# Attention blocks of a two-layer graph kernel on one core: 64-row transposes, another order of scores, context and projections, and three smaller edits

## What is computed

```python
# first layer: attention, then one of eight experts for each node
scores = einsum('bqhd,bkhd->bhqk', q, k) / sqrt(64)
attn = softmax(scores, axis=-1)
o = einsum('bqhk,bkhd->bqhd', attn, v).reshape(b, s, d) @ Wo + bo
h = layernorm(x + o, ln1_g, ln1_b)
probs = softmax(t @ gate_W + gate_b);  idx = argmax(probs);  gw = max(probs)
hid = gelu(einsum('nd,edf->enf', t, W1) + b1)        # 8 experts, 512 -> 2048
out = (einsum('enf,efd->end', hid, W2) + b2)[idx] * gw

# second layer, twice: attention along the edges (a segment softmax per target)
q = ((x @ Wq.T + bq) * 64 ** -0.5);  k = x @ Wk.T;  v = x @ Wv.T
w = segment_softmax(einsum('ehd,ehd->eh', q[tgt], k[src]), tgt)
agg = segment_sum(w * v[src], tgt)
```

## Time and profile before

| | us |
|---|---|
| median of 3 runs | 1137.88 (1135.78 to 1138.45) |
| the profiled execution: device time | 1139.18 |
| the profiled execution: span from first to last instruction | 1137.6 |
| PE busy in the span | 1087.7 |
| first attention, from its first projection | 234.5 to 377.5 |
| experts' loop | 407 to 640 |
| second and third attention | 650.5 to 787.7 and 853.5 to 989 |

### The profile page before, as it was taken

One profiled execution on the slowest core, in us unless ns is written; L12 is line 12 of the kernel. 1 busy time (PEld: TensorE's weight loads), 2 busy tenths in 40 slices (PEclk: granted clock), 3 DMA queues, 4 the chain that ended last, 5 costly groups with the idle time before them and its releaser, 6 DMA issues.

```text
span 1137.6 us, 20475 instructions
## 1 busy us (share of the span) xinstructions
PE 1087.7 (96%) x7489; PEld 733.2 (64%) x7490; DVE 561.7 (49%) x1409; ACT 373.8 (33%) x971; POOL 108.0 (9%) x145
## 2 busy tenths in 40 slices
PE   3899999999999989999999899999999999999999
PEld 2588746468777654455555577887577778755764
DVE  7898867745445422112211445453334555587641
ACT  1112222035455411122212345554124555412630
POOL 1000670020000021001101430000000000001000
PEclk9999999999999989999999999999999999999999
DMA  4100485000000369800799841000210000010001
GB/s 133 38 1 2 117 216 213 1 28 29 20 10 1 149 234 407 346 18 18 310 403 408 292 179 29 29 29 1 74 56 29 29 29 1 1 37 0 1 2 44
DMA packets 21405, 112.73 MB, mean 99 GB/s; under 512 B 5127, under 2 KB 6904, under 8 KB 15198
## 3 DMA queue, kind: packets, MB, share of 16 engines
q1 hardware_dynamic: 15864, 100.95, 23.6%
q0 software_dynamic: 5472, 10.83, 3.8%
HBM read 102.78 MB, written 8.98 MB: 98 GB/s over the span
## 4 chain that ended last, share of the span: by engine, by line
PE 85%; DMA 5%; DVE 4%; issue 3%; ACT 2%; POOL 1%; DVEq 0%; SPq 0%; POOLq 0%
PE psum L623 12%; PE psum L804 10%; PE psum L1003 7%; PE psum L971 6%; PE psum L827 6%; PE psum L858 6%; PE psum L809 5%; PE psum L840 5%; PE psum L691 4%; PE psum L1130 3%; PE psum L1034 3%; PE psum L641 3%; PE psum L1108 3%; DMA arena<-in_moeW 3%; PE psum L761 2%
## 5 line engine op out<-in xcount | busy, mean ns | idle before, releaser
L623 PE MATMUL psum<-arena 128*125 128x512 f32 x320 | 141.6, 599 | 0.8 <-ACT arena L1204 0.7
L1234 ACT ACTIVATE arena<-arena,small 125x625 f32<-125x625 f32 x120 | 97.0, 809 | 90.5 <-DVE small L1625 90.5
L804 PE MATMUL psum<-arena 128*128 128x313 f32 (+1 forms) x384 | 110.0, 435 | 2.3 <-ACT arena L1172 1.4
L1003 PE MATMUL psum<-arena 128*64 128x256 f32 x896 | 103.6, 390 | 5.1 <-DMA arena<-in_moeW 4.6
L623 PEld LDWEIGHTS psum<-arena 128*125 128x125 f32 x320 | 59.8, 190 | 74.7 <-issue 72.0
L1309 ACT ACTIVATE arena<-psum,cols 128x64 f32<-128x64 f32 x224 | 47.5, 363 | 183.8 <-PE psum L985 183.8
L971 PE MATMUL psum<-arena 128*64 128x512 f32 x448 | 99.2, 594 | 3.2 <-DMA arena<-in_moeW 2.2
L804 PEld LDWEIGHTS psum<-arena 128*128 128x128 f32 x384 | 70.0, 189 | 31.2 <-ACT arena L1172 2.5
L1003 PEld LDWEIGHTS psum<-arena 128*64 128x64 f32 x896 | 64.8, 140 | 38.7 <-issue 8.2
L1625 DVE CUSTOM_DVE_ANT_0 arena<-psum,cnt_adj 125x625 f32<-125x625 f32 x80 | 61.5, 806 | 54.9 <-PE psum L827 54.9
L1242 ACT ACTIVATE arena<-psum 125x500 f32<-125x500 f32 x120 | 63.8, 584 | 72.6 <-PE psum L840 72.6
(11 more groups left out here) (300 smaller groups left out, 1437.5 us busy)
## 6 DMA issues: line engine op xcount, KB each, us to landing
arena<-in_moeW SPq DMA_DIRECT2D x32, 2048.0 KB, 19.8
arena<-in_att SPq DMA_DIRECT2D x36, 256.0 KB, 2.7
arena<-in_l1W SPq DMA_DIRECT2D x2, 2048.0 KB, 12.1
token_rows<-arena POOLq DMA_DIRECT2D x19, 128.0 KB, 5.3
rows<-in_rows SPq DMA_DIRECT2D x1, 2240.0 KB
expert_rows<-arena POOLq DMA_DIRECT2D x17, 128.0 KB, 5.1
arena<-in_gnnWo SPq DMA_DIRECT2D x2, 1024.0 KB, 6.2
arena<-token_rows POOLq DMA_DIRECT2D x14, 128.0 KB, 6.6
```

What stands on the lines that cost most here:

```text
L623: mm = pe.matmul(bank(b, NP, D), srcT[:, k, c * NP:(c + 1) * NP], w[:, k, :], start=(k == 0), stop=(k == KC - 1))
L804: mm = pe.matmul(bank(b, P, width), aw[:, w, k, :], srcT[:, k, o:o + width], start=(k == 0), stop=(k == KC - 1))
L1003: mm = pe.matmul(psum[q * TT:(q + 1) * TT, 4 * 512:4 * 512 + D // 2], hT[:, f, :], EW2[par][:, f, q * (D // 2):(q + 1) * (D // 2)], start= ...
L1234: act.activation(Sx[u % 3][h], Sx[u % 3][h], ACT.Exp, bias=small[0:NP, 80 + n:81 + n], scale=-1.0, accum_out=small[0:NP, 120 + n:121 + n]) ...
```

## The change

Six things are changed.

1. `turned` works in pieces of 64 (or 61) query rows by 125 key columns, 20 instead of 10 for each unit. Rows 0 to 63 go to bank 3, rows 64 to 124 to bank 4, the tails to bank 7 (bank 5 in the last two units). The pieces alternate between the two row halves; one new semaphore, `low`, keeps two of them apart that write the same bank. `turned_out` copies them with two four-dimensional patterns and one plain one.
2. PE's order is scores(u+2), turned(u), context(u-1); the two last units keep the old order.
3. The six projection steps of the next pair stand together in the pair's third unit, between turned and context. The copies of q, k and v on ACT and DVE move to the same unit. Step 1 waits for the copied transposes, since both use bank 7, and the tails wait for the copied v.
4. DVE does largest(u+2) ahead of scaled(u+1). ACT does turned_out(u) ahead of exponentials(u+2).
5. The counting loops compare with the unmasked end; only the start is masked.
6. SP gives the second half of expert 1's first weights at once, and the wait (now for the scatter) stands behind it. PE waits for `xs` only behind the first half's transposes, in a one-column product that is added.

The core of the diff:

```diff
+QROWS = [(0, 64), (64, NP)]
+LAST = PAIRS * NC - 2
+BLOCK = 2
+def blocks_before(u):
+    return min(PAIRS, 1 + (u + NC - 1 - BLOCK) // NC)
+def tails_bank(u):
+    return 7 if u < LAST else 5
...
-            return [0] + [end & END_BITS for end in first], second
+            return [0] + [end & END_BITS for end in first], first, second
...
             first_weights(1, 1, 0)
-            sp.wait_ge(M["xs"], 16)
             first_weights(1, 1, 1)
+            sp.wait_ge(scattered, 16 * NC)
             sp.wait_ge(M["xsT"], 1)
...
-                with pe.Fori(ends[w], ends[w + 1], GT) as n:
+                with pe.Fori(starts[w], ends[w], GT) as n:
...
+                    def piece(g, h, j):
+                        r0, r1 = QROWS[g]
+                        o = 512 * (3 + g) + 64 * (4 * h + j) if j < 4 else 512 * tails_bank(u) + 64 * (2 * h + g)
+                        return pe.transpose(psum[0:NP, o:o + r1 - r0], Sx[u % 3][h][r0:r1, j * NP:(j + 1) * NP],
+                                            ident[r0:r1, r0:r1])
+                    for j in range(4):
+                        piece(0, 0, j)
+                        piece(1, 0, j)
+                    pe.wait_ge(s["prob"], 2 * u + 2)
+                    if u:
+                        pe.wait_ge(s["pTc"], 3 * u)
+                    if u < LAST:
+                        pe.wait_ge(s["vc"], 2 * blocks_before(u))
...
-                    if i + 1 < PAIRS:
-                        for n in ((0, 1), (2,), (3,), (4,), (5,))[c]:
+                    if u < LAST:
+                        turned(u)
+                    if c == BLOCK and i + 1 < PAIRS:
+                        for n in range(6):
+                            if n == 1:
+                                pe.wait_ge(s["pTc"], 3 * (u + 1))
                             projection(i + 1, n)
...
-                        pe.wait_ge(M["xs"], (g + 1) * 16)
...
                             if b == 0:
+                                pe.wait_ge(M["xs"], (g + 1) * 16)
+                                pe.matmul(bank(5, P, 1), xs[:, 0:P], ident[0:TT, 0:1], start=True, stop=True)
...
+                    if u + 2 < PAIRS * NC:
+                        largest(u + 2)
                     if u + 1 < PAIRS * NC:
                         scaled(u + 1)
-                    if u + 2 < PAIRS * NC:
-                        largest(u + 2)
```

More of the change, by code:

```diff
@@ L154, in build @@
         EW1_SIZE = KC * FF
-        AR = EW1_SIZE + 30893
+        AR = EW1_SIZE + 30909
         arena = sb("arena", [P, AR])
@@ L518, in _ @@
             pool.memset(twos[:], 2.0).then_inc(consts, 1)
-            pool.memset(gateW[:, KC * EX:], 0.0).then_inc(consts, 1)
-            pool.memset(gateW1[:, KC * EX:], 0.0).then_inc(consts, 1)
+            for h in range(2):
+                o = 2 * KC * EX + h * (WMIN // 2)
+                pool.memset(gates[:, o:o + WMIN // 2], 0.0).then_inc(consts, 1)
             pool.memset(zero_rows_sb, 0.0).then_inc(consts, 1)
@@ L667, in _ @@
             pe.wait_ge(range_ready, 1)
-            ends, shifts = window_ranges(pe, mybir.EngineType.PE)
+            starts, ends, shifts = window_ranges(pe, mybir.EngineType.PE)
             def window_banks(w):
@@ L1239, in turned_out @@
                         act.wait_ge(s["av"], u - 1)
[L1240 to L1243 removed]
+                    slot = u % 2 * NC
+                    for g in (1, 0):
+                        act.wait_ge(s["pT"], 3 * u + (1 if g else 3))
+                        n = QROWS[g][1] - QROWS[g][0]
+                        act.activation(PT[:, slot:slot + 4, :].rearrange("p j (h g n) -> p h j g n", h=2, g=2)[:, :, :, g, 0:n],
+                                       bank(3 + g, NP, 512).rearrange("p (h j n) -> p h j n", h=2, j=4)[:, :, :, 0:n],
                                        ACT.Copy).then_inc(s["pTc"], 1)
[L1245 to L1246 removed]
+                    act.activation(PT[:, slot + 4, :], bank(tails_bank(u), NP, 2 * P), ACT.Copy).then_inc(s["pTc"], 1)
                 act.activation(small[0:1, 95 + a:96 + a], onesf[0:1, 0:1], ACT.Exp)
@@ L1254, in attention @@
                     i, c = divmod(u, NC)
-                    if u >= PAIRS * NC - 2:
+                    if u >= LAST:
                         early(u - (PAIRS * NC - 1))
-                    if u:
+                    if u < LAST:
+                        turned_out(u)
+                    elif u > LAST:
                         turned_out(u - 1)
@@ L1260, in attention @@
                         exponentials(u + 2)
-                    if i + 1 < PAIRS:
-                        for n in ((0, 1), (2,), (3,), (), ())[c]:
+                    if c == BLOCK and i + 1 < PAIRS:
+                        for n in range(4):
                             projected(i + 1, n)
@@ L1509, in _ @@
             ve.wait_ge(range_ready, 1)
-            ends, shifts = window_ranges(ve, mybir.EngineType.DVE)
+            starts, ends, shifts = window_ranges(ve, mybir.EngineType.DVE)
             for w in range(NW):
-                with ve.Fori(ends[w], ends[w + 1], GT) as n:
+                with ve.Fori(starts[w], ends[w], GT) as n:
                     for s in range(GT):
@@ L1654, in attention @@
                     i, c = divmod(u, NC)
+                    if u + 2 < PAIRS * NC:
+                        largest(u + 2)
                     if u + 1 < PAIRS * NC:
                         scaled(u + 1)
-                    if u + 2 < PAIRS * NC:
-                        largest(u + 2)
-                    if i + 1 < PAIRS and c >= 3:
-                        values(i + 1, c + 1)
+                    if c == BLOCK and i + 1 < PAIRS:
+                        values(i + 1, 4)
+                        values(i + 1, 5)
                     if u >= PAIRS * NC - 2:
```

54 lines of the change are left out of this document (28 added, 26 removed).

## The result

The changed kernel takes **1123.97 us** (median of 4 runs, 1123.75 to 1124.71), the kernel before 1137.68 in the same comparison: a ratio of 0.9895, 95% interval 0.9876 to 0.9914. That is 13.7 us less, where 42.5 were forecast, and 1.97 us above the end of the range. The profiled execution has a span of 1123.2 us, and by its page PE is busy for 1072.3 of them (95%), DVE for 557.9 and ACT for 371.0 (this answers to the earlier trace rows). PE still bounds. Where the time went is best seen by stage.

What follows compares the result with a forecast made beforehand. PE was taken to bound the kernel; attentions 38.5, experts 2.0 and loops 2.0 sum to 42.5 us, taking 1137.88 to 1095.4 us. Range 1085 to 1122, main case 1085 to 1100 with chance 0.58.

Steps and rivals of the forecast that it cites:

- Transposes: Attentions: 20 pieces take 0.61 us, saving 0.57 in each of 54 units; with the last units 33.0 us.
- The overlap of the halves: Pieces on the two row halves of PE run beside each other, so 20 pieces cost 10 x 0.061 us.
- each half pays a full load: Rival, attention transposes: ten pieces in each half take 1.04 us, 26 us more in all, 1121; chance 0.05.
- the halves do not overlap: Rival, attention transposes: 20 pieces take 20 x 0.061 = 1.22 us, giving 1130; chance 0.08.
- Change of section between scores and pieces: Attention units: none counted, as both use the same row halves; rival that it stays: 10.8 us, 1106, chance 0.07.
- Projections in a block: Attentions: five sections in each pair become one, saving 36 x 0.22 = 7.9 us.
- Start of each attention: PE waits about 1.0 us before scores(3) and some 0.2 for turned(0); costs 3 x 1.2 = 3.6 us.
- The last two units: End of each attention: units keep their place behind the context and save 0.37 us each, six times.
- DVE as the bound: Rival: DVE or ACT bounds units without projections, 0.2 us more for 15 units per attention, 9 us, 1104; chance 0.10.
- Experts: Expert stretch: earlier weights gain 4.0 us, the added one-column product costs 2.0; net 2.0 us gained.
- The wait for `xs`: Experts: PE's 3.24 us wait for first rows could become 0.9 shorter or 3 longer; nothing taken.
- Loops: Counting loops: one register operation less at each of 37 passes, 0.055 us each, 2.0 us, between 0 and 2.6.

Runs made afterwards that it cites:

- the second run: Changed kernel plus 13 rows of otherwise useless products by the identity behind the last attention, twelve 512-column products ahead of each row: 1300.32 us.

## Why the prediction was wrong

- **Transposes: 33.0 forecast, 10.8 in the ordinary units. This is the step that failed.** It took the price of a piece from the experts', 0.06 us, and said that "only 125 for 128 columns and two full halves for one and a half differ". The 125 columns were the difference: 0.109 against 0.062 a piece on one half. The overlap of the halves, on which I thought that most would hang, is complete. The rival with the right mechanism was "each half pays a full load" (1121 us, chance 0.05); I gave it little since the earlier trace rows spoke against it, without a row of my own shape. The rival "the halves do not overlap" names nearly the right price for 20 pieces (1.22, measured 1.18) for the wrong reason. With 128 columns the unit takes 3.24 us (forecast 3.20), and with the tails first 3.11, and 3.15 in the mean.
- **What the rows before could have told.** The prediction read a price by rows out of the earlier trace rows, 0.06 for 128 columns in 64 rows and 0.11 in 125. But rows 6 are plain products and rows 4 transposes, and that is the difference: the load of 128 columns lasts 140 ns in transposes of 64 and of 125 rows, and 192 in the plain product. And the load records of the kernel before already had 125 columns as the dearer load: 188 ns for the full transposes of the attentions, 153 in the mean for the experts' pieces with 128 columns, some of which ran at the lower clock. Groups by line, shapes apart, before:

```profile
L840 PEld LDWEIGHTS psum<-ident,arena 125*125 125x125 f32 x480 | 57.1, 188 | 10.0 <-issue 9.5
L985 PEld LDWEIGHTS psum<-ident,arena 64*128 64x128 f32 x224 | 15.7, 153 | 0.0
```

- **Change of section between scores and pieces.** It is gone, as forecast: scores and transposes together took 2.55 us and now take 2.35, though the loads cost the same; with full transposes in the new order it is 2.55 again.
- **Projections in a block: 7.9 forecast, 6.8 measured**, all projections of an attention 55.2 before and 52.9 now, no idle time in a block.
- **Start of each attention: 1.2 forecast, 1.0 measured** in the first: pieces 1.91 instead of 1.18 and scores(2) 1.44 instead of 1.17, with a wait of 0.54 for the maxima. The trace:

```profile
247.58 1.34 PE L841 MATMUL psum<-arena 64*125 64x113 f32 x8
249.02 1.36 PE L852 MATMUL psum<-ident,arena 64*125 64x64 f32 x20
250.93 1.34 PE L841 MATMUL psum<-arena 64*125 64x113 f32 x8 [0.54 <-DVE small L1668]
```

- **The last two units: 2.2 forecast as a gain, some 3.8 measured as a loss.** The first attention has 1.0 more in these units' pieces, the two others 0.34 more (1.36 twice against 1.19 twice) and the new wait of 1.07 each. I had priced them as the others. The order of their waits is another: 12 pieces behind the context's copy, and the first early product behind a copy that DVE does after a scaling. This was not in the forecast at all.
- **DVE as the bound (rival, 0.10)** did not come in the changed kernel, whose unit is 3.57 us. The spare time was as thin as the rival said: at 3.24 DVE has 0.18 left, and with the tails first, at 3.15 in the mean, the pieces start on the end of DVE's scaling.
- **Experts: 2.0 gain forecast, 0.4 loss measured.** The waits for weights went (4.0, right in kind). The wait for `xs` was put at 0.9 shorter or 3 longer, and nothing taken; it became 4.7 longer. The bound was drawn for a scatter that shares the engines. It was the read-back behind it that did, since the change releases 4 MB of weights by the same signal that releases it.
- **Loops: 2.0 forecast (0 to 2.6), 3.9 to 4.6 measured.** I priced one register operation a pass, 0.040 us and a step. One goes from DVE's list and one from PE's for each pass, 93 to 56 of them on each engine, and 0.105 went. Which of the two carries it was not tried.

## What to carry to other kernels

When a price is taken from another place in a trace, take it from the same shape in all of its numbers, columns of the load included, or measure it alone; here three columns decided 16 us. Where a wait is swapped for an earlier signal, ask what else that signal releases, and let the small transfer that an engine waits for go ahead of the large one. And after a step has been made faster, look at the waits inside it: with 0.109 us a pair the `low` wait cost nothing that can be seen (ten pairs and 0.09), with 0.062 it cost 0.13 us a unit. The new limit can be another engine, as DVE was here.

## What the runs showed of the hardware

- Float32 transposes of 64 rows start 0.109 us apart with 125 columns to load, 0.062 with 128 and 0.057 with 96; their load records last 186, 140 and 123 ns. A plain float32 product with 128 columns has a load record of 192. Pieces on the two row halves in alternation run beside each other, a pair costs what one costs; with all of one half ahead of the other it was 2.44 us instead of 1.52.
- The granted clock fell to 0.50 in a row of short transposes with no idle time between them, PE 100% busy by the profile, and in the second run in the products of 512 columns right behind the first such row (992 to 994). It was 1.00 in all rows of the second run that are used here, and in the attentions with fast pieces.
- A read of 128 KB from DRAM landed 2.5 us after its issue alone and 7.0 us after it beside 4 MB of weights.
